# Causal attention with a bias table: the tiles of queries of a chunk of heads taken from the last to the first

## The chip, the cores and the metric

The kernel runs on one core of one Trainium2 chip. The metric is the time of one execution on the device, in microseconds (us). The core has five engines that run beside each other, each through its own list of instructions in order, and that wait for one another by counting semaphores: TensorE (PE in the profile, with its weight loads as PEld), ScalarE (ACT), VectorE (DVE), GpSimd (POOL) and SyncE (SP), which starts the transfers.

## The reference

The reference is a decoder of four layers over 4 sequences of 512 tokens of width 128. Each layer has an attention, a cross attention to 154 tokens of context and a feed-forward part, each followed by a layer norm. The change touches one of these twelve parts, the attention of the last layer (16 heads of width 8; the kernel runs it with a table for 512 positions):

```python
def _L3_attn_ref(x, WQ, bQ, WK, bK, WV, bV, WO, bO, rel_pos_table):
    q = (x @ WQ.T + bQ).reshape(b, t, N_HEADS, D_K).transpose(0, 2, 1, 3)
    k = (x @ WK.T + bK).reshape(b, t, N_HEADS, D_K).transpose(0, 2, 1, 3)
    v = (x @ WV.T + bV).reshape(b, t, N_HEADS, D_K).transpose(0, 2, 1, 3)
    scores = jnp.einsum('bhqd,bhkd->bhqk', q, k) / jnp.sqrt(jnp.float32(D_K))
    ...
    scores = scores + rel_bias.transpose(2, 0, 1)[None]
    causal = pos[None, :] <= pos[:, None]
    scores = jnp.where(causal[None, None], scores, -jnp.inf)
    attn = jax.nn.softmax(scores, axis=-1)
    out = jnp.einsum('bhqk,bhkd->bhqd', attn, v)
    out = out.transpose(0, 2, 1, 3).reshape(b, t, d)
    return out @ WO.T + bO
```

Because of the causal mask, a tile of 128 queries needs only the keys up to its own end: the first tile 128 keys, the second 256, the third 384, the last 512.

## The kernel before

The program loops twice over pairs of sequences. Within a pass it goes through the parts of the network, and each part is done for one sequence ("lane") and then for the other. The attention with the table (class `L3Attention`, lines 2181 to 2233) thus runs four times in an execution; each of these runs is called a stage below.

A stage first projects queries, keys and values (`pe_table`, line 338) and then runs an object of class `Attention` (line 465), which serves all the softmax attentions of the network. For this stage it has 16 heads in four chunks of four heads (`hpc` is 4: each head has a strip of 32 partitions), and four rounds for a chunk (`rpc` is 4), each with one tile of 128 queries (`nq` and `w` are 1). So there are 16 rounds, and a round has four items k = 0 to 3, one for each head. `width` (line 521) gives the keys of an item: 128 times the number of the query tile, counted from one.

The rounds are pipelined over 18 steps. In step i each engine does, in this order:

- PE: the scores of round i (line 561, each head into a PSUM bank of its own, the head's matmul waiting until VectorE has read that bank in the round before); at the first step past a chunk's last round the transposes of the reciprocals (line 572); the transposes of the probabilities of round i-1 (line 592), the four heads going through a ring of three PSUM banks, so that a head's transposes wait until the bank's last content has been copied out; the products with the values of round i-2 (line 610), all into bank O1.
- DVE: per head, scores plus bias, written to NB with the row minimum of the negated sum (line 719, which waits for the scores); between the heads' instructions the reciprocal of the sums (line 734) and the copies of two heads of round i-1 (line 640); at the end of the step behind a chunk's last products the multiplication of the chunk's output by the reciprocals (line 745), which waits for those products. PE's first products of the next chunk wait for it.
- ACT: per head the exponential (line 691, which also sums the row), and the copies of the other two heads of round i-1 (line 638); once a chunk the copy of the transposed reciprocals (line 647).
- POOL: the spreading of the reciprocals over the strips (line 656).

In rounds 0 and 1 PE issues a matmul whose result nobody reads just ahead of the first transposes (`warm=(0, 1)`, `idle` at lines 399 and 586). In step 1 DVE also does the layer norm of the sequence before (`beside`, line 2232), and in step 3 PE transposes the input of the next stage (`late={3: ["X"]}`, line 804), which ACT copies in step 4 (line 813). In the last step PE does the output projection of the first two chunks, then the last products, then the projection of chunks 3 and 4 (line 754).

The tile of queries of a round is `rd % self.rpc` in four places: `item` (line 518), the products (line 606), the spreading (line 651) and the reciprocal (line 733). So a chunk goes through 128, 256, 384 and 512 keys, and the next chunk starts again with 128.

Of the kernel before, what the change touches and what calls it, by code (L numbers as in the profile page):

```python
# [13 lines left out]
P = 128  # L14
NBATCH, SEQ, CTX = 4, 512, 154
# [185 lines left out]
def build(nc, io):  # L201
    ctx = ExitStack()
    with ctx:
# [261 lines left out]
        class Attention:  # L465
# [1 line left out]


            def __init__(self, heads, dh, nkeys, added=None, causal=False, keys=None, queries=None,
                         banks=None, split="ADDA", exes=None, late=None, warm=(), turn_first=True):  # L470
                self.heads, self.dh, self.nkeys, self.added, self.causal = heads, dh, nkeys, added, causal
                self.keys, self.queries = keys, queries
                self.ctx = nkeys == CTX
                self.kc = CK if self.ctx else P
                self.nch = nkeys // self.kc
                self.slot = {8: 32, 64: 64, P: P}[dh]
                self.hpc = P // self.slot
                self.chunks = heads // self.hpc
                self.w = 2 if self.ctx else 1
                self.nq = 4 * self.w // self.hpc  # L480
                self.rpc = NT // self.nq
                self.rounds = self.chunks * self.rpc
                self.banks = banks or PP3
                self.exes = exes or [EX[:, e, :] for e in range(4)] + [QT[:, 4 + e, :] for e in range(4)]
                self.steps = self.rounds + 2
                self.seq, self.first = [], []
                self.late = late or {}
                self.x_done = None
                self.warm = warm
                self.turn_first = turn_first  # L490
                self.late_at = {}
                done = {"A": 0, "D": 0}
                self.also(0)
                self.recip_at = []
                for rd in range(self.rounds + 1):
                    if rd >= 1 and rd % self.rpc == 0:
                        self.recip_at.append(len(self.seq))
                        done["A"] += 1
                        self.seq.append(("A", done["A"]))
                    self.first.append(len(self.seq))  # L500
                    for k in range(4 if rd < self.rounds else 0):
                        done[split[k]] += 1
                        self.seq.append((split[k], done[split[k]]))
                    self.also(rd + 1)
# [7 lines left out]
            def late_bank(self, j):  # L512
                return self.banks[self.late_at[j] % len(self.banks)]

            def item(self, rd, k):

                q, j = divmod(k, self.hpc)
                q0 = (rd % self.rpc) * self.nq + q * self.w
                return list(range(q0, q0 + self.w)), j

            def width(self, qts):
# [22 lines left out]
            def pe(self, pe, r, ready=(), beside=None, wo=None, fill=None, valued=(), late=None, fill_at=1):  # L544
                nb = len(self.banks)
                for i in range(self.steps):
                    if i == fill_at and fill:
                        fill(pe)
                    if i < self.rounds:
                        rd, c = i, i // self.rpc  # L550
# [47 lines left out]
                    if 0 <= rd < self.rounds:  # L598
                        c = rd // self.rpc
                        for k in range(4):  # L600
                            self.evacuated(pe, r, self.first[rd] + k)
                        if rd % self.rpc == 0 and c >= 1:
                            pe.wait_ge(r.av_sb, c)
                        for sem, count in valued if rd == 0 else ():
                            pe.wait_ge(sem, count)
                        q0 = (rd % self.rpc) * self.nq
                        last = q0 if self.causal else self.nch - 1
                        for kc in range(last + 1):
                            for j in range(self.hpc):
                                ins = pe.matmul(O1[self.slot * j:self.slot * (j + 1), q0 * P:(q0 + self.nq) * P],  # L610
                                                self.value(c * self.hpc + j, kc), self.probs(rd, j)[:, kc, :],
                                                start=(kc == 0), stop=(kc == last))
                        ins.then_inc(r.av, 1)
# [34 lines left out]

            def spread(self, pool, r, rd):

                c, q0 = rd // self.rpc, (rd % self.rpc) * self.nq
                pool.wait_ge(r.recip, rd + 1)
                if c >= 1:
                    pool.wait_ge(r.recipT, c)
                of = recips[:, self.column(c, q0, 0, self.nq * self.hpc)]
                pool.tensor_copy(RX[:, q0 * P:(q0 + self.nq) * P].rearrange("p (n s) -> p n s", s=self.slot),  # L656
                                 of.unsqueeze(2).broadcast_to([P, self.nq * self.hpc, self.slot])
                                 ).then_inc(r.spread, 1)
# [41 lines left out]
            def dve(self, dve, r, free=None, beside=None, late=None):  # L700
                for i in range(self.steps):
                    for j in self.late.get(i - 1, ()):
                        if j != "X":
                            late(dve, j)
                    for k in range(4):
                        if i < self.rounds:
                            rd = i
                            n = 4 * rd + k
                            qts, j = self.item(rd, k)
                            h, N = (rd // self.rpc) * self.hpc + j, self.width(qts)  # L710
                            dve.wait_ge(r.scores, n + 1)
                            if self.added and rd >= 1:
                                dve.wait_ge(r.exped, n - 3)
                            elif n >= 8:
                                dve.wait_ge(r.exped, n - 7)
                            at = 2 * (n % 8)
                            if self.added:
                                for a, qt in enumerate(qts):
                                    ins = dve.tensor_tensor_reduce(  # L719
                                        NB[:, k, a * N:(a + 1) * N], S4[k][:, a * N:(a + 1) * N],  # L720
                                        self.added(h, qt), -1.0, HUGE, ALU.add, ALU.min, neg[:, at + a:at + a + 1])
                            else:
                                ins = dve.tensor_reduce(neg[:, at:at + self.w],
                                                        S4[k][:, 0:self.w * N].rearrange("p (a k) -> p a k", k=N),
                                                        AX.X, ALU.max, negate=True)
                            ins.then_inc(r.negmax, 1)
                        if 1 <= i <= self.rounds and k >= 2:
                            rd, c = i - 1, (i - 1) // self.rpc
                            if k == 2:
                                dve.wait_ge(r.exped, 4 * rd + 4)  # L730
                                if c >= 2:
                                    dve.wait_ge(r.spread, (c - 1) * self.rpc)
                                of = self.column(c, (rd % self.rpc) * self.nq, 0, self.nq * self.hpc)
                                dve.reciprocal(recips[:, of], sums[:, of]).then_inc(r.recip, 1)  # L734
                                self.turn(dve, r, "D", rd, 0, free)
                                self.turn(dve, r, "D", rd, 1, free)
                            else:
                                self.turn(dve, r, "D", rd, 2, free)
                                self.turn(dve, r, "D", rd, 3, free)
                    rd = i - 2  # L740
                    if 0 <= rd < self.rounds and rd % self.rpc == self.rpc - 1:
                        c = rd // self.rpc
                        dve.wait_ge(r.av, rd + 1)
                        self.evacuated(dve, r, self.recip_at[c])
                        dve.tensor_tensor(self.out_chunk(c), O1[:, :], RS[:, c % 2, :], ALU.mult).then_inc(r.av_sb, 1)  # L745
                    if beside:
                        beside(i)
# [1433 lines left out]
        class L3Attention(LaneStep):  # L2181
            kind = 13

            def __init__(self, *a):
                LaneStep.__init__(self, *a)
                w, XT = self.w, self.L.XT
                self.att = Attention(16, 8, SEQ, causal=True, keys=lambda c: KT[:, c, :],
                                     added=lambda h, qt: relbias[:, h, SEQ - P * (qt + 1):SEQ], warm=(0, 1),
                                     late={3: ["X"]})
                rowsA = [([(w("wq")[:, c * P:(c + 1) * P], XT[:, :])], P, SEQ, "A", "act", QT[:, c, :],  # L2190
                          (ACT.Identity, scaled[:, 4 + c:5 + c], RSQRT8)) for c in range(4)]
# [363 lines left out]
```

## Time and profile before

| what | us |
|---|---|
| median of 3 runs | 4173.82 |
| lowest, highest run | 4170.47, 4176.15 |
| the profiled execution | 4180.67 |
| its span from first to last instruction | 4179.0 |
| busy in the span: PE, DVE, ACT, POOL | 3893.9, 2766.9, 1978.4, 948.6 |
| mean granted TensorE clock | 0.977 |

The profiled execution is a run of its own, 6.85 us above the median of the three. A time read from its rows is a place or a length within its span of 4179.0 us. PE's busy time counts a matmul from its start to its modelled end, and the matmuls overlap, so that a row such as "x8" with 1.09 us holds eight of them.

### The profile page before, as it was taken

How to read it: one execution, taken by the hardware profiler on the slowest of the kernel's cores; microseconds unless marked ns; L12 is line 12 of the kernel's file. 1: busy time of each engine (PE TensorE's matmuls, PEld its weight loads, DVE VectorE, ACT ScalarE, POOL GpSimd, SP SyncE). 2: the span in 40 equal slices, each digit the busy share in tenths (PEclk: the TensorE clock that was granted, in tenths of full speed). 3: DMA queues.
4: the chain of work that ended last, by engine and by line, in shares of the span. 5: the costliest groups of instructions: out<-in, count | busy, mean ns of one | idle time of the engine just before them, and what ended most of it. 6: DMA issues, size and time to landing. Idle time of an engine off the chain costs nothing. (4 is left out here: it accounts for less than half of the span.)

```text
span 4179.0 us, 70765 instructions
## 1 busy us (share of the span) xinstructions
PE 3893.9 (93%) x23508; PEld 2394.3 (57%) x23508; DVE 2766.9 (66%) x8036; ACT 1978.4 (47%) x5740; POOL 948.6 (23%) x1040
## 2 busy tenths in 40 slices
PE   7999899999999999999989998999999999999998
PEld 4644455665655655666646444565556556555665
DVE  3787767677767747664447886776777776476644
ACT  1732445655555533663228224555565555346722
POOL 0145332233322200000001462322323321000000
PEclk8999999999999999999979999999999999999999
DMA  1100000000000010000010000000000000201000
GB/s 57 43 17 1 17 7 18 24 17 24 17 24 2 26 58 21 31 37 9 4 59 6 17 1 17 7 17 24 18 24 17 24 2 26 72 7 56 12 9 11
DMA packets 15853, 91.87 MB, mean 22 GB/s; under 512 B 2176, under 2 KB 8064, under 8 KB 12032
## 3 DMA queue, kind: packets, MB, share of 16 engines
q1 hardware_dynamic: 15488, 87.27, 5.8%
q8 instruction: 196, 3.21, 0.3%
q14 instruction: 169, 1.38, 0.1%
HBM read 86.22 MB, written 1.05 MB: 21 GB/s over the span
## 5 line engine op out<-in xcount | busy, mean ns | idle before, releaser
L610 PE MATMUL ps_O<-wide,V 128*64 128x256 f32 (+4 forms) x5152 | 596.2, 393 | 1.9 <-ACT wide L638 1.9
L691 ACT ACTIVATE EX<-NB,neg 128x154 f32<-128x154 f32 (+3 forms) x768 | 402.7, 531 | 107.6 <-DVE neg L719 107.6
L561 PE MATMUL ps_S<-KT,QT 64*128 64x154 f32 (+7 forms) x1936 | 373.5, 456 | 59.9 <-POOL QT L1619 25.3
L656 POOL COPY RX<-recips 128x256 f32<-128x256 f32 (+2 forms) x356 | 156.6, 440 | 1127.9 <-DVE recips L734 1127.9
L745 DVE TENSOR_TENSOR QT<-ps_O,RS 128x512 f32<-128x512 f32 x212 | 146.5, 691 | 395.2 <-PE ps_O L610 394.6
L640 DVE COPY wide<-ps_P 128x512 f32<-128x512 f32 (+4 forms) x528 | 339.8, 647 | 75.2 <-PE ps_P L592 72.4
L610 PEld LDWEIGHTS ps_O<-wide,V 128*64 128x64 f32 (+4 forms) x5152 | 266.8, 127 | 194.6 <-issue 110.7
L429 POOL TENSOR_TENSOR small<-small 128x4 f32<-128x4 f32 x112 | 113.6, 1014 | 1065.6 <-DVE small L414 902.8
L561 PE MATMUL ps_T<-KT,QT 64*128 64x154 f32 (+5 forms) x968 | 322.2, 435 | 3.4 <-ACT EX L691 3.4
L561 PE MATMUL ps_OUT<-KT,QT 64*128 64x154 f32 (+5 forms) x968 | 325.2, 434 | 0.1
L592 PE MATMUL ps_P<-consts,EX 128*128 128x128 f32 (+1 forms) x1956 | 294.1, 286 | 25.9 <-ACT RS L647 13.0
L691 ACT ACTIVATE QT<-NB,neg 128x512 f32<-128x512 f32 (+2 forms) x512 | 311.8, 619 | 0.0
L561 PEld LDWEIGHTS ps_S<-KT,QT 64*128 64x128 f32 (+2 forms) x1936 | 159.2, 188 | 249.8 <-issue 163.0
L638 ACT ACTIVATE wide<-ps_P 128x512 f32<-128x512 f32 (+4 forms) x432 | 241.2, 558 | 124.7 <-PE ps_P L592 124.5
L592 PEld LDWEIGHTS ps_P<-consts,EX 128*128 128x128 f32 (+1 forms) x1956 | 226.6, 149 | 78.1 <-ACT RS L647 21.4
L592 PE MATMUL ps_P<-consts,QT 128*128 128x128 f32 (+1 forms) x1624 | 240.3, 280 | 24.5 <-DVE wide L640 11.1
L592 PEld LDWEIGHTS ps_P<-consts,QT 128*128 128x128 f32 (+1 forms) x1624 | 177.6, 143 | 87.6 <-issue 36.8
L638 ACT ACTIVATE wide<-ps_O 128x512 f32<-128x512 f32 (+2 forms) x280 | 160.1, 572 | 112.8 <-PE ps_O L592 112.8
L561 PEld LDWEIGHTS ps_OUT<-KT,QT 64*128 64x128 f32 (+2 forms) x968 | 155.2, 189 | 80.3 <-issue 68.0
L719 DVE CUSTOM_DVE_ANT_0 NB<-ps_S,maskb 128x512 f32<-128x512 f32 x256 | 165.9, 685 | 40.8 <-PE ps_S L561 40.8
L754 PEld LDWEIGHTS ps_OUT<-weights,QT 128*128 128x128 f32 x1536 | 178.3, 192 | 24.8 <-issue 24.8
L754 PE MATMUL ps_OUT<-weights,QT 128*128 128x128 f32 x1536 | 190.4, 278 | 0.0
(388 smaller groups left out, 8231.5 us busy)
## 6 DMA issues: line engine op xcount, KB each, us to landing
weights<-in_w_dram SPq DMA_DIRECT2D x10, 1664.0 KB, 6.9
weights<-in_w_dram SPq DMA_DIRECT2D x2, 6148.0 KB, 17.5
weights<-in_w5next_dram SPq DMA_DIRECT2D x6, 1664.0 KB, 6.9
weights<-in_w_dram SPq DMA_DIRECT2D x2, 4200.0 KB, 12.9
weights<-in_reltab_dram SPq DMA_DIRECT2D x2, 4096.0 KB, 14.1
weights<-in_w_dram SPq DMA_DIRECT2D x8, 640.0 KB, 3.9
weights<-in_w_dram SPq DMA_DIRECT2D x5, 832.0 KB, 4.5
weights<-in_w_dram SPq DMA_DIRECT2D x2, 2050.0 KB, 7.9
```

Source lines behind the costliest of these rows:

```text
L429: pool.tensor_tensor(small[:, 36:40], small[:, 32:36], small[:, half:half + 4], ALU.pow).then_inc(r.rstd, 1)
L561: ins = pe.matmul(S4[k][:, a * N:(a + 1) * N], QT[strip, c, qts[a] * P:(qts[a] + 1) * P], self.keys(c)[strip, 0:N], start=True, stop=True)
L592: ins = pe.transpose(self.banks[s % nb][0:self.kc, b * P:(b + 1) * P], ex[:, a * N + kc * self.kc:a * N + (kc + 1) * self.kc], ident)
L610: ins = pe.matmul(O1[self.slot * j:self.slot * (j + 1), q0 * P:(q0 + self.nq) * P], self.value(c * self.hpc + j, kc), self.probs(rd, j)[:, ...
L638: eng.activation(dst, src, ACT.Copy).then_inc(r.turned_act, 1)
L640: eng.tensor_copy(dst, src).then_inc(r.turned_dve, 1)
L656: pool.tensor_copy(RX[:, q0 * P:(q0 + self.nq) * P].rearrange("p (n s) -> p n s", s=self.slot), of.unsqueeze(2).broadcast_to([P, self.nq * ...
L691: ins = act.activation(ex[:, a * N:(a + 1) * N], src, ACT.Exp, bias=neg[:, at:at + 1], scale=-1.0 if self.added else 1.0, accum_out=sums[: ...
L719: ins = dve.tensor_tensor_reduce(NB[:, k, a * N:(a + 1) * N], S4[k][:, a * N:(a + 1) * N], self.added(h, qt), -1.0, HUGE, ALU.add, ALU.min ...
L745: dve.tensor_tensor(self.out_chunk(c), O1[:, :], RS[:, c % 2, :], ALU.mult).then_inc(r.av_sb, 1)
L754: ins = pe.matmul(OUT[:, t * P:(t + 1) * P], self.out_chunk(c)[:, t * P:(t + 1) * P], wo[:, c * P:(c + 1) * P], start=(c + t == 0), stop=( ...
```

## The change

`Attention` gets an option `down`. With it, round n of a chunk takes query tile 3-n in place of n: a chunk begins with the tile of 512 keys, goes on with 384 and 256 and ends with 128. The function `query` gives the tile to the four places that computed it, and `L3Attention` alone sets the option. The number of instructions, their sizes, the buffers, the waits and the order of the kinds of work in a step remain; only which round is how wide changes.

```diff
             def __init__(self, heads, dh, nkeys, added=None, causal=False, keys=None, queries=None,
-                         banks=None, split="ADDA", exes=None, late=None, warm=(), turn_first=True):
+                         banks=None, split="ADDA", exes=None, late=None, warm=(), turn_first=True,
+                         down=False):
...
+            def query(self, rd):
+
+                n = rd % self.rpc
+                return (self.rpc - 1 - n if self.down else n) * self.nq
+
             def item(self, rd, k):
 
                 q, j = divmod(k, self.hpc)
-                q0 = (rd % self.rpc) * self.nq + q * self.w
+                q0 = self.query(rd) + q * self.w
                 return list(range(q0, q0 + self.w)), j
...
-                        q0 = (rd % self.rpc) * self.nq
+                        q0 = self.query(rd)
                         last = q0 if self.causal else self.nch - 1
...
-                c, q0 = rd // self.rpc, (rd % self.rpc) * self.nq
+                c, q0 = rd // self.rpc, self.query(rd)
...
-                                of = self.column(c, (rd % self.rpc) * self.nq, 0, self.nq * self.hpc)
+                                of = self.column(c, self.query(rd), 0, self.nq * self.hpc)
...
                 self.att = Attention(16, 8, SEQ, causal=True, keys=lambda c: KT[:, c, :],
-                                     added=lambda h, qt: relbias[:, h, SEQ - P * (qt + 1):SEQ], warm=(0, 1),
+                                     added=lambda h, qt: relbias[:, h, SEQ - P * (qt + 1):SEQ], warm=(0, 1), down=True,
                                      late={3: ["X"]})
```

## Rows read from the trace of the kernel before

**Rows 1.** Stage two: stretch, us, busy PE, PEld, DVE, ACT, POOL, clock, DMA.

```profile
1704.88:1768.12 63.24, 58.86 (x666) 38.89 (x667) 46.75 (x185) 49.20 (x165) 4.69 (x16) 1.00 0.01 2
```

**Rows 2.** The same view for one chunk in the middle of stage one.

```profile
1652.23:1666.28 14.05, 13.01 (x160) 8.34 (x164) 11.21 (x45) 12.10 (x42) 1.17 (x4) 1.00 0.00 1
```

**Rows 3.** Who waited for whom in that chunk: us in total, times, longest.

```profile
PEld ps_P L592 <- ACT wide L638: 1.0, 2, 0.8
DVE NB L719 <- PE ps_T L561: 1.0, 1, 1.0
DVE QT L745 <- PE ps_O L610: 0.9, 1, 0.9
```

**Rows 4.** Timeline of that chunk, PE: start, us, engine, line, instruction, count.

```profile
1652.09 0.59 PE L561 MATMUL ps_S<-KT,QT 32*128 32x384 f32 x2
...
1652.95 0.44 PE L592 MATMUL ps_P<-consts,QT 128*128 128x128 f32 x2
...
1654.23 0.43 PE L610 MATMUL ps_O<-wide,V 128*32 128x128 f32 x8
...
1654.59 0.70 PE L561 MATMUL ps_S<-KT,QT 32*128 32x512 f32 x2
...
1658.14 0.64 PE L610 MATMUL ps_O<-wide,V 128*32 128x128 f32 x16
1658.72 0.38 PE L561 MATMUL ps_S<-KT,QT 32*128 32x128 f32 x2
...
1659.28 1.09 PE L592 MATMUL ps_P<-consts,QT 128*128 128x128 f32 x8
...
1661.92 0.86 PE L610 MATMUL ps_O<-wide,V 128*32 128x128 f32 x24
...
1662.72 0.48 PE L561 MATMUL ps_S<-KT,QT 32*128 32x256 f32 x2
...
1663.36 0.66 PE L572 MATMUL ps_P<-consts,RX 128*128 128x128 f32 x4
...
1665.13 1.08 PE L610 MATMUL ps_O<-wide,V 128*32 128x128 f32 x32
1666.14 0.59 PE L561 MATMUL ps_S<-KT,QT 32*128 32x384 f32 x2
```

**Rows 5.** The same timeline, DVE: scores plus bias of 512 and of 256 keys.

```profile
1655.75 0.69 DVE L719 CUSTOM_DVE_ANT_0 NB<-ps_S,weights 128x512 f32<-128x512 f32 x1
...
1656.36 0.68 DVE L719 CUSTOM_DVE_ANT_0 NB<-ps_S,weights 128x512 f32<-128x512 f32 x1
...
1663.45 0.42 DVE L719 CUSTOM_DVE_ANT_0 NB<-ps_S,weights 128x256 f32<-128x256 f32 x1 [1.03 <-PE ps_T L561]
```

**Rows 6.** Timeline of stage two's start: first scores, unread matmul, first chunk's multiplication.

```profile
1704.88 0.38 PE L561 MATMUL ps_S<-KT,QT 32*128 32x128 f32 x2 [0.43 <-issue]
...
1707.10 1.12 PE L402 MATMUL ps_P<-consts 128*128 128x512 f32 x2
...
1708.06 0.38 PE L592 MATMUL ps_P<-consts,EX 128*128 128x128 f32 x2
...
1724.10 0.69 DVE L745 TENSOR_TENSOR QT<-ps_O,RS 128x512 f32<-128x512 f32 x1 [0.90 <-PE ps_O L610]
```

**Rows 7.** Busy time in stage one from third to fourth multiplication, and behind it.

```profile
1680.33:1694.34 14.01, 13.28 (x153) 8.91 (x154) 8.29 (x27) 9.04 (x26) 0.88 (x3) 1.00 0.00 1
1694.34:1696.25 1.91, 1.91 (x17) 1.91 (x18) 1.28 (x2) 0.00 (x0) 0.00 (x0) 1.00 0.00 0
```

**Rows 8.** Busy time and clock, first scores to first multiplication: stages two, one, three, four.

```profile
1704.88:1724.10 19.22, 17.64 (x188) 11.37 (x192) 14.76 (x67) 15.97 (x58) 1.46 (x5) 1.00 0.01 3
1631.86:1652.23 20.37, 18.94 (x188) 11.84 (x192) 14.64 (x67) 15.94 (x58) 1.46 (x5) 0.92 0.01 2
3713.24:3733.51 20.27, 18.80 (x188) 11.49 (x192) 14.58 (x67) 15.85 (x58) 1.46 (x5) 0.92 0.01 2
3786.17:3806.99 20.82, 19.39 (x188) 12.09 (x192) 14.76 (x67) 15.97 (x58) 1.46 (x5) 0.92 0.01 2
```

More of the change, by code:

```diff
@@ L490, in __init__ @@
                 self.turn_first = turn_first
+                self.down = down
                 self.late_at = {}
```

## The prediction

> **What bounds the kernel now.** I read the busy time over whole stages first. Stage two takes 63.24 us from its first scores to the end of its projection [rows 1]; there are four such stages in the execution, and outside them the program is the same. Next I read a single chunk. In its steady state a chunk takes 14.05 us, and in it PE is busy for 13.01, ACT for 12.10 and DVE for 11.21 [rows 2]. PE's figure counts matmuls that overlap, so what PE issues has to be taken from the starts of its groups. Then the waits: none is long, but they sit on different engines, 1.0 us of DVE for scores, 0.9 of DVE for the chunk's last products, 1.0 of PE's weight loads for a copy by ACT [rows 3]. So no engine is full, and the period is a ring in which each engine waits a little for the next. Last the timeline of PE, which gives each step its length. I write a step as (scores; transposes; products) in tiles of 128 keys. From one first scores matmul to the next, (3;2;1) takes 2.50 us, (4;3;2) 4.13, (1;4;3) 4.00 and (2;1;4) 3.42, which sums to 14.05 [rows 4].
>
> **The parts of a step, from rows.** Scores hold PE for 0.64 us at two tiles (1662.72 to 1663.36) and 0.86 at three (1652.09 to 1652.95), 0.22 a tile; so 0.43 at one and 1.08 at four. Transposes cost 0.11 each (eight in 1.09, of which the last one's tail is 0.2). Products take 0.36, 0.58, 0.80 and 1.01 us for one to four tiles (to the next first scores) [rows 4]. DVE starts on scores of four tiles 1.16 us after they start, and goes on every 0.61 us [rows 4, 5]; its result counts 0.7 us after its start.
>
> **The change, part by part.** Nothing is removed or added: the same instructions of the same sizes run in another order of rounds. The steps become (4;1;2), (3;4;1), (2;3;4), (1;2;3). POOL and the transfers have nothing on this path: POOL is busy for 1.17 us of a chunk [rows 2], and no DMA of a stage moves. I lay each step out along PE.
>
> - (4;1;2): scores 1.08, four transposes 0.44, a wait of 0.5 for a copy by ACT before the fourth head's transposes may use the ring (the kind in [rows 3]), products 0.58. Sum 2.60.
> - (3;4;1): each head's scores need DVE to have read the four-tile scores of the same head. The last of these reads starts 1.22 (1.16 and the semaphore) + 3 x 0.61 + 0.27 (a reciprocal and a one-tile copy between them) after the four-tile scores began, and counts 0.74 later: 4.06, so 1.46 into this step. Then 0.86 scores, 0.55 transposes of the reciprocals, 1.90 for 16 transposes with two short waits, 0.36 products. Sum 5.13. This is the step that gets worse: the wide reads of DVE stand bare here, while before PE met them with the transposes of three tiles.
> - (2;3;4): scores 0.72, twelve transposes and a wait for ACT's copy 2.07, products 1.01. Sum 3.80.
> - (1;2;3): scores 0.45, eight transposes with a wait 1.24, products 0.80. Sum 2.49.
>
> The chunk sums to 14.02 us, against 14.05 [rows 2]. Two full periods lie between a stage's first and third multiplication, so they give 0.06 us back.
>
> Start of a stage. Before, 19.22 us lie between the first scores and the first multiplication, at full clock [rows 6, 8]. After: DVE has read the last four-tile scores at 1.22 + 3 x 0.61 + 0.74 = 3.79; three-tile scores 0.86, to 4.65; the unread matmul 0.96 (1707.10 to 1708.06 in [rows 6]), to 5.61; 16 transposes 1.90, to 7.51; two-tile scores, behind a 0.44 wait for DVE, which has the four-tile copies to make, to 8.59; unread matmul to 9.55; twelve transposes 1.56 and products 1.01, to 12.12; (1;2;3) with the four transposes of the next stage's input 2.93, to 15.05; (4;1;2) to 17.65; (3;4;1) to 22.78; multiplication 0.54 later, 23.32. This costs 4.10 us a stage.
>
> End of a stage. Before, the third and fourth multiplications are 14.01 us apart and the projection ends 1.91 later [rows 7]. After, counted from the third multiplication: the step (2;3;4) began 0.54 earlier, so 3.80 - 0.54 = 3.26; (1;2;3) 2.49; one-tile transposes with their waits 1.07, products of two tiles 0.58; reciprocals 0.44; half the projection 1.87; the last products, now of one tile, and the step over to DVE 0.54. Sum 10.25, which gives back 3.76 us. What follows the multiplication stays 1.91.
>
> A stage: +4.10 - 0.06 - 3.76 = +0.28 us, four of them +1.1 us. The long start is paid by the short end, since a pipeline's start costs its first rounds and its end its last ones, and the sizes only swap places.
>
> The clock. In stage two the granted clock stays at 1.00 (2.4 GHz) during the start; in the other three it falls to 1.2 GHz for a part of it (mean 0.92), and these starts take 20.37, 20.27 and 20.82 us against 19.22, so a fall costs 1.15, 1.05 and 1.60, 3.8 us in all [rows 8]. PE ran short bursts of scores just before. After the change PE has scores alone for 4.65 us, with 0.9 us of nothing in them, so I take falls in three or four stages. At half clock the unread matmul (0.96) and the 16 wide transposes (1.76) may double: a fall costs between 1.05, the cheapest row, and 2.7; I take 1.7, nearest to the dearest row. 3.5 x 1.7 - 3.8 = +2.2 us.
>
> Sum: +1.1 + 2.2 = +3.3 us. On the profiled span 4179.0 becomes 4182.3, with the 1.67 us around it 4184.0; that execution lies 6.85 above the median, and the median of 4173.82 becomes 4177.
>
> **The rivals.** F, faster. The chunk's end is what binds the ring: DVE waits 0.90 us for the chunk's last products [rows 6] and then 1.03 for scores [rows 5]. The last products shrink from 1.01 to 0.36 us, and in my working the multiplication no longer waits. If this were the path, 0.9 us for each of 16 chunks would go: 14.4, 4159. Against it: in the new order DVE waits instead for the one-tile scores behind the four-tile products (0.8) and for the four-tile scores (1.6), so the idle moves.
>
> S, slower, by the clock. The fall does not stay at the stage's start. In (3;4;1) PE again has little but scores, held apart by DVE's reads, for some 2.3 us. If that brings the clock down once in every chunk, 16 falls at the mean of the three rows, 1.27, make 20.3 in place of 3.8: +16.5 + 1.1, 4191. For it: the three falls at the starts. Against it: the one-tile and two-tile transposes and products run between, and the chunk before keeps 1.00 throughout [rows 2]. It decides as soon as the low stretch recurs in each chunk. The Trainium skill, page "TensorE: Matmul & The Clock Gate", section "HAM oscillation", says that a loop whose waits recur in each pass can have its clock lowered in each pass. By that rule S would hold; the trace of before agrees for starts only.
>
> T, slower: the end gives nothing back, because ACT or DVE and not PE ends it: then +3.76 x 4 = 15.0 on top of 3.3, 4192. Against it: behind the last multiplication PE is busy for 1.91 of 1.91 us [rows 7], and ACT has no work there.
>
> **How the numbers follow.** Forecast 0.68, F 0.12, S 0.13, T 0.07. The forecast's own range is 4168 to 4186: half a microsecond to one and a half on each stage for the waits that I only estimated, and 1.05 to 2.7 for a fall in two to four stages. A measurement of this kernel can tell about 0.2% from no change, 8.3 us. The forecast gives 0.01 faster, 0.59 the same and 0.08 slower; F gives faster; S and T give slower but for a fall in only a few chunks, which stays within. Range 4166 to 4192. Faster 0.13, same 0.60, slower 0.27.
>
> **What would show each step.** Multiplications (line 745) 14.0 us apart within a stage; the first 23.3 us (full clock) behind the first scores; the fourth 10.25 behind the third; steps of 2.6, 5.1, 3.8 and 2.5 us. DVE's 0.90 wait ahead of line 745 gone, and a wait of some 1.6 us ahead of the first four-tile read of a chunk. Whole stages of 63.5 to 66 us. I would be wrong if the period differs by more than 0.3 us, for there are twelve of them, or if the granted clock in mid-stage is below 1.00.

## The result and the profile after

The changed kernel takes 4186.21 us (median of 13 runs, 4178.07 to 4194.06) against 4173.82 before (13 runs, 4164.34 to 4182.62). The ratio is 1.003, with a 95% interval from 1.0021 to 1.004: slower by 0.2 to 0.4%. Timed a second time it was 1.0021 (1.0011 to 1.0031). The forecast was 4177 with a range of 4166 to 4192, and "within 0.2%" as the likeliest case. The time lies in the whole range, 9 us above the point and on the slower side of the bound, but at the very edge of what the forecast itself allowed (4168 to 4186): the room up to 4192 came from the rivals S and T.

Busy time over the four stages in the profile after. Columns: stretch, us, busy time of PE, PEld, DVE, ACT and POOL with their instructions, granted clock, share of DMA, GB/s.

```profile
1629.13:1695.14 66.01, 63.06 (x665) 41.14 (x666) 45.70 (x185) 49.77 (x165) 4.73 (x16) 0.95 0.01 2
1703.77:1769.96 66.19, 63.19 (x666) 41.22 (x667) 45.80 (x185) 49.82 (x165) 4.73 (x16) 0.95 0.01 2
3721.61:3787.57 65.96, 63.00 (x665) 41.19 (x666) 45.73 (x185) 49.72 (x165) 4.73 (x16) 0.95 0.01 2
3796.20:3862.42 66.22, 63.25 (x666) 41.20 (x667) 45.79 (x185) 49.81 (x165) 4.73 (x16) 0.95 0.01 2
```

They sum to 264.4 us. In the first profile of the kernel before, the four stages took 64.39, 63.24, 64.30 and 64.83, together 256.8 ([rows 1] is the second of them). So the stages account for +7.6 of the +11.4 us between the two spans, 4190.4 and 4179.0. The rest lies in parts that the change does not touch. ACT, DVE and POOL are busy for as long as before within 1 us; PE is busy for longer, and its mean clock is 0.95 in all four stages.

The same view from the first scores to the first multiplication (line 745 of before, 752 of after), stage two first, for [rows 8]:

```profile
1703.77:1729.89 26.12, 25.03 (x204) 15.18 (x204) 17.29 (x68) 18.05 (x56) 1.48 (x5) 0.87 0.01 2
1629.13:1655.08 25.95, 24.91 (x204) 15.13 (x204) 17.22 (x68) 18.00 (x56) 1.47 (x5) 0.87 0.00 1
3721.61:3747.51 25.90, 24.85 (x204) 15.18 (x204) 17.26 (x68) 17.94 (x56) 1.48 (x5) 0.87 0.00 1
3796.20:3822.34 26.14, 25.09 (x204) 15.20 (x204) 17.27 (x67) 18.04 (x56) 1.48 (x5) 0.87 0.01 2
```

Then one period, the way from the third to the fourth multiplication and what follows it, all of stage two, for [rows 2, 7]:

```profile
1729.89:1743.81 13.92, 13.31 (x163) 8.45 (x156) 10.91 (x47) 12.23 (x42) 1.19 (x4) 1.00 0.01 2
...
1757.73:1768.05 10.32, 9.64 (x140) 7.23 (x134) 5.40 (x27) 7.32 (x28) 0.89 (x3) 1.00 0.01 2
1768.05:1769.97 1.92, 1.92 (x18) 1.92 (x19) 1.29 (x2) 0.00 (x0) 0.00 (x0) 1.00 0.00 0
```

The period of 13.92 us, the short end of 10.32 and the unchanged 1.92 are what the steps gave (14.02, 10.25, 1.91). The start is not: 26 us against 23.3. The timeline of PE shows the steps of the period by their first scores, for [rows 4], and that of DVE its two longest waits for scores and the multiplication without a wait, for [rows 5]:

```profile
1729.41 0.48 PE L568 MATMUL ps_S<-KT,QT 32*128 32x256 f32 x2
...
1733.20 0.38 PE L568 MATMUL ps_S<-KT,QT 32*128 32x128 f32 x2
...
1735.71 0.70 PE L568 MATMUL ps_S<-KT,QT 32*128 32x512 f32 x2
...
1738.32 0.91 PE L568 MATMUL ps_S<-KT,QT 32*128 32x384 f32 x4
...
1743.33 0.48 PE L568 MATMUL ps_S<-KT,QT 32*128 32x256 f32 x2
```

```profile
1733.72 0.29 DVE L726 CUSTOM_DVE_ANT_0 NB<-ps_S,weights 128x128 f32<-128x128 f32 x1 [0.79 <-PE ps_T L568]
...
1736.87 0.69 DVE L726 CUSTOM_DVE_ANT_0 NB<-ps_S,weights 128x512 f32<-128x512 f32 x1 [1.48 <-PE ps_T L568]
...
1743.81 0.68 DVE L752 TENSOR_TENSOR QT<-ps_O,RS 128x512 f32<-128x512 f32 x1
```

The steps take 3.79, 2.51, 2.61 and 5.01 us. Last, the start of stage two in PE's timeline, for [rows 6], and the clock of 6.7 us in it:

```profile
1703.77 0.70 PE L568 MATMUL ps_S<-KT,QT 32*128 32x512 f32 x2 [0.43 <-issue]
...
1709.11 2.07 PE L402 MATMUL ps_P<-consts 128*128 128x512 f32 x2
...
1710.98 1.92 PE L599 MATMUL ps_P<-consts,EX 128*128 128x128 f32 x8
...
1714.53 0.48 PE L568 MATMUL ps_S<-KT,QT 32*128 32x256 f32 x2
...
1715.17 1.13 PE L402 MATMUL ps_P<-consts 128*128 128x512 f32 x2
```

```profile
1707.70:1714.40 6.70, 6.70 (x21) 4.29 (x20) 2.84 (x11) 3.30 (x11) 0.29 (x1) 0.50 0.00 1
```

The unread matmul comes 5.34 us behind the first scores (worked out: 4.65), the transposes at 7.21 (5.61) and the next scores at 10.76 (7.51). Of these 3.25 us, 0.44 are won back, since the wait for DVE that my steps had among these scores is gone. From the second unread matmul on (11.40, worked out 8.59) the distance to my steps is 2.8 us and stays. All of the loss lies in a stretch that PE spends at half clock.

### The profile page after: what moved, and what is told of

The parts are those of the page before. It is cut to its first block and busy times, and to the rows that moved or that the text cites. A ratio compares the mean times of both kernels' runs of the same rounds, so it can differ in the third digit from the quotient of the medians.

```text
span 4190.4 us, 70765 instructions
## 1 busy us (share of the span) xinstructions
PE 3908.6 (93%) x23508; PEld 2401.7 (57%) x23508; DVE 2764.0 (66%) x8036; ACT 1982.3 (47%) x5740; POOL 950.2 (23%) x1040
## 3 DMA queue, kind: packets, MB, share of 16 engines
HBM read 86.22 MB, written 1.05 MB: 21 GB/s over the span
## 5 line engine op out<-in xcount | busy, mean ns | idle before, releaser
L698 ACT ACTIVATE EX<-NB,neg 128x154 f32<-128x154 f32 (+2 forms) x768 | 416.5, 549 | 113.7 <-DVE neg L726 113.7
L599 PE MATMUL ps_P<-consts,EX 128*128 128x128 f32 (+1 forms) x2048 | 307.9, 289 | 22.4 <-ACT RS L654 9.2
L698 ACT ACTIVATE QT<-NB,neg 128x512 f32<-128x512 f32 (+3 forms) x512 | 298.1, 592 | 0.0
L599 PEld LDWEIGHTS ps_P<-consts,EX 128*128 128x128 f32 (+1 forms) x2048 | 241.0, 150 | 68.5 <-issue 21.5
L599 PE MATMUL ps_P<-consts,QT 128*128 128x128 f32 (+1 forms) x1536 | 231.0, 281 | 23.5 <-DVE wide L647 11.1
L645 ACT ACTIVATE wide<-ps_O 128x512 f32<-128x512 f32 (+3 forms) x280 | 159.4, 569 | 113.1 <-PE ps_O L599 112.2
```

The source lines that it names most:

```text
L599: ins = pe.transpose(self.banks[s % nb][0:self.kc, b * P:(b + 1) * P], ex[:, a * N + kc * self.kc:a * N + (kc + 1) * self.kc], ident)
L645: eng.activation(dst, src, ACT.Copy).then_inc(r.turned_act, 1)
L698: ins = act.activation(ex[:, a * N:(a + 1) * N], src, ACT.Exp, bias=neg[:, at:at + 1], scale=-1.0 if self.added else 1.0, accum_out=sums[: ...
```

## The experiments

Theory C: the start is longer than the steps say because the granted clock is at 1.2 GHz for 6.8 us there. Rival D: waits for DVE and ACT make it longer, and the clock is a bystander. The other runs test the terms of the sum, the start, the end and the joins, one at a time. "Stages" is the sum of the four stages in the run's own profile.

| kernel | median, us | ratio to before (95%) | stages, us |
|---|---|---|---|
| before, again (x_before) | 4175.19 | 1.0003 (0.9992 to 1.0013) | 255.6 |
| changed (first series) | 4186.21 | 1.0030 (1.0021 to 1.0040) | 264.4 |
| changed, again (x_after) | 4183.50 | 1.0021 (1.0011 to 1.0031) | 263.5 |
| changed, four unread matmuls more (x_keep) | 4188.37 | 1.0034 (1.0021 to 1.0047) | 266.9 |
| changed, one unread matmul more (x_fill) | 4170.33 | 0.9989 (0.9980 to 0.9998) | 255.4 |
| changed, without unread matmuls (x_nowarm) | 4169.11 | 0.9985 (0.9975 to 0.9996) | 252.4 |
| first chunk down only (x_first) | 4186.89 | 1.0026 (1.0015 to 1.0038) | 266.6 |
| last chunk down only (x_last) | 4166.67 | 0.9981 (0.9972 to 0.9991) | 244.8 |
| up, down, up, down (x_zigzag) | 4151.17 | 0.9953 (0.9940 to 0.9965) | 237.4 |
| x_zigzag, one half-size unread matmul more (x_zigfill) | 4148.31 | 0.9940 (0.9926 to 0.9954) | 234.7 |
| x_zigfill, without the unread matmuls of rounds 0 and 1 (x_zigbare) | 4150.35 | 0.9944 (0.9924 to 0.9964) | 230.9 |
| before, without unread matmuls (x_upbare) | 4170.44 | 0.9986 (0.9975 to 0.9997) | 252.6 |

**Four unread matmuls (x_keep).** In `Attention.pe`, ahead of the wait of line 559:

```diff
+                                    if rd == 1 and self.down:
+                                        n = SEQ if k == 0 else SEQ // 2
+                                        pe.matmul(self.banks[0][:, 0:n], ident, K("cos")[:, 0:n], start=True, stop=True)
```

> The changed kernel with unread matmuls put between the scores of round 1 (one of 512 columns ahead of the first head's, one of 256 ahead of each other head's), so that PE does not stand still while DVE reads the wide scores. Theory C (the start of a stage is 2.7 us longer than my 23.3 because the granted clock is at half for 6.8 us there): the clock stays at 1.00 in the start, the first multiplication comes 23.5 to 24.5 us behind the first scores instead of 26.0, a stage takes about 64.2 instead of 66.1, and the kernel 8 us less than the changed one, near 4178. Rival D (the start is long by the waits for DVE and ACT themselves, and the clock is a bystander): the clock comes back, but the first multiplication stays at 26 us or later, since matmuls were only added, and the time stays at 4186 or above.

In three of the four stages the clock stayed at 1.00, and the start still took 25.96 us, as D has it. But the edit was no clean test of D. PE's timeline of stage two shows that the full-width matmuls keep the heads' scores from running beside each other:

```profile
1629.18:1657.97 28.79, 28.60 (x212) 16.43 (x212) 17.47 (x67) 18.04 (x56) 1.46 (x5) 0.88 0.00 1
1706.66:1732.62 25.96, 25.77 (x212) 14.60 (x212) 17.35 (x67) 17.93 (x56) 1.46 (x5) 1.00 0.01 2
```

```profile
1708.79 0.91 PE L571 MATMUL ps_S<-KT,QT 32*128 32x384 f32 x2
1709.63 0.70 PE L567 MATMUL ps_P<-consts 128*128 128x256 f32 x2
1710.26 0.91 PE L571 MATMUL ps_S<-KT,QT 32*128 32x384 f32 x2
1711.10 0.70 PE L567 MATMUL ps_P<-consts 128*128 128x256 f32 x2
```

Head follows head every 1.47 us, where DVE alone would let them go every 0.61. What the clock gave back, the added work took, so the 25.96 us say nothing for D. The first stage (the upper of the two windows) speaks for C: it had a fall of 6.8 us in spite of the added matmuls, and with the same instructions its start took 2.83 us longer than the other three.

**One unread matmul (x_fill).** Only the one that falls into a wait of PE is kept:

```diff
+                                    if rd == 1 and k == 0 and self.down:
+                                        idle(pe, self.banks[0])
```

> The changed kernel with a single unread matmul of 512 columns added, ahead of the first head's scores of round 1, where PE stands still for 0.85 us at full clock; nothing is added between the other heads' scores. Theory C (half clock makes the start 2.8 us longer than the steps say): the clock no longer falls for 6.8 us in the start, or for 3.4 at most, the first multiplication comes 23.3 to 23.7 us behind the first scores where the clock stays at 1.00, and a stage takes 63.6 to 64 there in place of 66.1; with all four so, -8 to -10 us against the changed kernel, 4176 to 4178. Rival D (waits make it, the clock is a bystander): the clock stays up and the first multiplication still comes at 26 us.

```profile
1703.04:1726.30 23.26, 23.07 (x206) 13.72 (x206) 17.17 (x68) 17.93 (x56) 1.46 (x5) 1.00 0.01 2
1630.04:1654.54 24.50, 24.31 (x202) 15.26 (x206) 17.25 (x67) 18.60 (x58) 1.46 (x5) 0.93 0.00 1
3749.00:3764.20 15.20, 14.58 (x159) 10.01 (x156) 11.00 (x46) 12.78 (x44) 1.17 (x4) 0.89 0.01 2
```

```profile
1704.11 1.12 PE L402 MATMUL ps_P<-consts 128*128 128x512 f32 x2
...
1707.71 1.12 PE L402 MATMUL ps_P<-consts 128*128 128x512 f32 x2
1708.67 1.04 PE L601 MATMUL ps_P<-consts,EX 128*128 128x128 f32 x8
...
1710.54 0.48 PE L570 MATMUL ps_S<-KT,QT 32*128 32x256 f32 x2
```

The edit only adds work on PE, and yet the start shrinks from 26 to 23.26 us in three of the four stages: C holds and D falls. The added matmul puts the next scores only 0.13 us later (2.13 us behind the first scores, 2.00 in the changed kernel), since it stands in a wait. The unread matmul of round 0 stands at 4.67 us behind the first scores, the transposes at 5.63 and the next scores at 7.50, where my steps had 4.65, 5.61 and 7.51. Two of the four stages took 63.32 us at full clock. The other two had one fall of 3.4 us each, not ahead of the first transposes but later, at 20 and at 48 us behind the first scores, and took 64.37. The second row of the windows is the start with the first of these, 24.50 us; the last row is the other, a period of 15.20 us instead of 13.91.

**No unread matmuls (x_nowarm)**, in `L3Attention`:

```diff
-    warm=(0, 1), down=True,
+    warm=(), down=True,
```

> The changed kernel without the two unread matmuls of rounds 0 and 1. They took 1.87 us at half clock and 0.97 at full clock, and in the changed order both stand on PE's path. If they only cost (theory C, with the low stretch where it was): the first multiplication comes at 23.2 to 23.5 us instead of 26.1, the kernel is 10 us below the changed one, 4176. If they are what brings the clock back (the low stretch gets longer without them): 24.5 to 27 us. Rival D, in which PE waits there for DVE and ACT anyway: 25.5 to 26 us with an unchanged low stretch.

```profile
1696.79:1720.25 23.46, 22.42 (x200) 14.65 (x200) 17.35 (x68) 18.05 (x56) 1.46 (x5) 0.85 0.01 2
1625.47:1648.10 22.63, 21.58 (x200) 13.71 (x200) 17.16 (x67) 18.04 (x56) 1.46 (x5) 0.92 0.01 1
```

All four starts still have a fall, of 6.8 us in two stages and of 3.4 in the other two, and they take 2.5 to 3.5 us less than in the changed kernel. So in this order the two matmuls stand on PE's path and did not keep the clock up. They came after the stretch in which PE had only scores. No start of this run was at full clock, so what they cost there is not shown by it (x_zigbare against x_zigfill below: 0.9 us, 19.87 against 20.79, in the other order).

**The first chunk alone (x_first)**, with `query` asking whether the chunk is in a list, and `down=(0,)`:

```diff
-                return (self.rpc - 1 - n if self.down else n) * self.nq
+                return (self.rpc - 1 - n if rd // self.rpc in self.down else n) * self.nq
```

> The kernel before with only the first chunk of each stage from 512 down to 128, the other three up. It has the changed start and the old end. Working by steps at full clock: first multiplication 19.9 us behind the first scores (0.7 more than before), periods 14.05 and 14.01 as before, so +0.7 a stage, about +3 us. Theory C adds the long half-clock stretch: 2.7 us on each start against about 1.0 before: first multiplication near 22.5, +2.3 to +2.9 a stage, 4183 to 4186. Rival D: the start is slower by waits alone, first multiplication also above 22 us but with the clock at 1.00.

```profile
1706.55:1729.11 22.56, 21.15 (x188) 13.24 (x192) 14.40 (x68) 15.54 (x55) 1.46 (x5) 0.85 0.01 2
```

All four starts took 22.5 to 22.8 us with a fall of 6.8 us in each, 2.6 to 2.9 above the 19.9 of the steps (which no run measured at full clock), the periods 14.05 and the ends 14.0. Turning the first chunk alone is enough to bring the long fall. It is not the only way to one: two starts of x_upbare below have it with narrow first rounds.

**The last chunk alone (x_last)**, with the same `query`:

```diff
-    warm=(0, 1), down=True,
+    warm=(0, 1), down=(3,),
```

> The kernel before with only the last chunk of each stage from 512 down to 128. It has the old start and the changed end. By the steps: the join of two rounds of 512 keys costs 1.4 us (third multiplication 15.5 behind the second in place of 14.05), the fourth follows 10.1 to 10.3 later in place of 14.01, net -2.4 us a stage, -9 to -10 us: 4164. Under rival T (the end gives nothing back) the kernel would stay at 4174 or above; the trace of the changed kernel speaks against T already.

```profile
1662.74:1678.04 15.30, 15.26 (x172) 9.86 (x176) 14.10 (x45) 14.04 (x43) 1.19 (x4) 1.00 0.01 2
1678.04:1688.18 10.14, 9.88 (x141) 7.43 (x142) 5.29 (x26) 7.13 (x26) 0.89 (x3) 1.00 0.01 2
```

The join of two rounds of 512 keys costs 1.25 us, the end gives back 3.9, and the kernel is faster by 0.1 to 0.3%. The gain at the end is real and does not hang on the start.

**Up, down, up, down (x_zigzag)**, with the same `query`:

```diff
-    warm=(0, 1), down=True,
+    warm=(0, 1), down=(1, 3),
```

> Chunks one and three up (128 to 512), chunks two and four down (512 to 128): the old start, the changed end, two joins of 512 to 512 keys and one of 128 to 128. By the steps the first multiplication is at 20.9 (its chunk's last step stands beside wider scores), then 10.4, 15.5 and 10.1: about 58.7 us a stage at full clock against 63.2, so -4 to -4.6 a stage and -16 to -18 us: 4156 to 4158. If joins cost more than the steps say, or the clock falls at them, -8 us or less.

```profile
1624.70:1645.50 20.80, 19.98 (x200) 12.88 (x204) 17.36 (x68) 18.01 (x58) 1.46 (x5) 1.00 0.01 2
1645.50:1656.00 10.50, 9.85 (x148) 6.67 (x152) 8.05 (x46) 9.62 (x39) 1.17 (x4) 1.00 0.01 2
1656.00:1671.29 15.29, 15.25 (x172) 9.85 (x176) 14.09 (x45) 14.56 (x46) 1.17 (x4) 1.00 0.01 3
1671.29:1681.43 10.14, 9.89 (x141) 7.43 (x142) 5.30 (x27) 7.12 (x26) 0.88 (x3) 1.00 0.01 2
```

The rows meet the steps (20.9, 10.4, 15.5, 10.1) to 0.2 us each, and the kernel beats both the one before, by 0.35 to 0.6%, and the changed one. Two of its four starts had a fall of 3.4 us and took 22.1 us instead of 20.8. Here both ends of a stage meet a small round, and the turning points are 512 to 512 and 128 to 128 instead of 512 to 128.

**Two variants of it (x_zigfill, x_zigbare).** The first adds an unread matmul of 256 columns ahead of round 1's first scores, the second has that one and drops those of rounds 0 and 1.

```diff
+                                    if rd == 1 and k == 0 and self.down:
+                                        pe.matmul(self.banks[0][:, 0:256], ident, K("cos")[:, 0:256], start=True, stop=True)
...
-    warm=(0, 1), down=(1, 3),
+    warm=(), down=(1, 3),
```

> The kernel with chunks one and three up and two and four down, plus an unread matmul of 256 columns ahead of the first head's scores of round 1. Where the clock fell for 3.4 us in the start (two stages of four) a stage took 1.3 us more than where it did not (60.0 against 58.7). Theory C: no fall in the four starts, every stage 58.7 to 58.9, some 2 us less in the four together, too little for the timed ratio: 4149 to 4151. If the fill costs more than it saves: 59.2 or more in each stage.

> Chunks up, down, up, down, with the added unread matmul of 256 columns ahead of round 1 but without the two of rounds 0 and 1. With them the four stages took 58.6 to 58.7 us with the clock at 1.00. Path theory: 0.7 to 1.0 us less each where the clock stays up, 57.7 to 58.0, so 4144 to 4146. Clock theory: one or more of the four starts has a fall of 3.4 or 6.8 us, stages of 59 to 60 there, and nothing is gained: 4148 to 4152.

```profile
1692.36:1751.07 58.71, 57.39 (x668) 38.96 (x669) 46.32 (x185) 49.35 (x165) 4.74 (x16) 1.00 0.01 2
```

```profile
1630.30:1688.02 57.72, 56.59 (x663) 38.59 (x664) 45.86 (x185) 49.23 (x165) 4.69 (x16) 1.00 0.01 2
```

None of these eight stages had a fall: 58.6 to 58.7 us each, then 57.7. The three intervals of this order overlap, so the timed runs do not rank them.

**The kernel before without unread matmuls (x_upbare).**

```diff
-    added=lambda h, qt: relbias[:, h, SEQ - P * (qt + 1):SEQ], warm=(0, 1),
+    added=lambda h, qt: relbias[:, h, SEQ - P * (qt + 1):SEQ], warm=(),
```

> The kernel before (all chunks up) without its two unread matmuls. In the changed order taking them away gave 2.5 to 3.4 us a stage. In the old order the steps say: the first matmul stands between the scores of round 1 and the first transposes, the second partly beside a wait for DVE, so at full clock 0.5 to 0.8 us a stage; if a start then has the 6.8 us fall as in the changed kernel, +1.5 in place of it. Path theory: 3 us faster, 4171. Clock theory (they earn their place by keeping the clock up in the old order): the falls get longer, stages at 65 or more, 4177 or above.

```profile
1631.45:1651.09 19.64, 18.25 (x184) 11.70 (x188) 14.50 (x68) 15.97 (x58) 1.48 (x5) 0.83 0.01 2
3712.44:3730.99 18.55, 17.01 (x184) 11.35 (x188) 14.39 (x67) 15.97 (x58) 1.48 (x5) 0.91 0.01 2
```

The falls did get longer (6.8 us in two stages, 3.4 in the others), and still no start took more than 19.64 us, where before they took 19.2 to 20.8. The path theory was nearer, in time and size; of the clock theory only the longer falls came.

**The controls (x_before, x_after)**, the two kernels without an edit.

> The kernel before once more, as a control of the comparison: ratio 1.000 with an interval of about 0.001 to each side, periods 14.05, ends 14.0 and 1.9, stages of 63.2 without and 64.3 to 64.8 with a fall of the clock in the start. How many of the four starts have a fall is open (three in the first profile); it tells how much of the stages' +7.6 us between the two first profiles is chance: 1.2 us for each.

> The changed kernel once more. The four stages took 7.6 us more than in the first profile of the kernel before and 8.8 more than in its second, while the medians are 12 us apart; this run tells whether the remaining 3 to 4 us are chance. If the stages are all: ratio 1.0020, about 4182, and a second profile with 66.0 to 66.2 us in each stage and 3917 to 3922 outside them. If something outside the stages is slower too: ratio 1.003 again and 3925 or more outside them.

The kernel before, run again, had two falls in its four starts, where its first profile had three, and stages of 255.6 us. The changed kernel, timed again, came to 1.0021. Three of its starts had the 6.8 us fall and took 25.8 to 27.0 us, one had 3.4 us and took 24.6:

```profile
3791.81:3816.42 24.61, 23.57 (x204) 14.56 (x204) 17.17 (x67) 17.93 (x56) 1.47 (x5) 0.93 0.01 2
```

So the start grows with the length of the fall: 23.26 us without one (x_fill), 24.6 with 3.4 us, 26.0 with 6.8. The start of 27.0 us, in the third stage, had a second fall of 3.4 us on top. The stages sum to 263.5 us, and the time outside them was 3921 us, as in the other profiles (3908 to 3926).

## Why the prediction was right or wrong

**The order of the steps.** Right, term by term. At full clock (x_fill) the start took 23.26 us (23.32 worked out), the period 13.91 (14.02), the end 10.32 (10.25), the rest 1.91. Against before that is +4.04, two times -0.14 and -3.69, so +0.1 us a stage: 63.32 against 63.24, where I had +0.28. "The long start is paid by the short end" holds to a tenth of a microsecond at full clock. One slip in the signs of being wrong: there are not twelve periods but eight, two in each stage; the third distance is the end.

**The step that gets worse.** (3;4;1) took 5.01 us, against 5.13. DVE's 0.90 us wait for the last products is gone, and 1.48 and 0.79 us of waiting for scores stand in its place (I had 1.6 and 0.8). So rival F was a shift of idle time, as argued: the period fell by 0.13 us and not by 0.9.

**The clock, the term that was mis-sized.** I expected falls in three or four stages at 1.7 us each, 6.0 in all. They came in all four of the first profile at 26.03 - 23.26 = 2.8 us each, 11.1 in all. The range I gave for one fall, 1.05 to 2.7, ended just below that. I took the value nearest to the dearest row of before, 1.60, but those rows were falls of 3.4 us over narrow transposes, and after the change a fall lasts 6.8 us and covers the unread matmul (1.87 instead of 0.96) and the 16 wide transposes with their waits (3.55 instead of 1.90). Both were named in the prediction as what "may double"; the value should have gone to that end. Comparisons within one kernel agree: 2.83 us for 6.8 us of half clock in x_keep, and 1.2 to 1.4 us between a fall of 3.4 and one of 6.8 in x_after. With 11.1 in place of 6.0 the sum is 0.4 + 11.1 - 3.8 = +7.7, which is the +7.6 of the stages.

**From the stages to the median.** The first series has 12.4 us between the medians, the second 10.8, and the ratio of the second, 1.0021, is +8.8. The stages give 7.6 to 8.8, by which profile of before is taken. The interval of the second series (4.6 to 12.9 us) holds these, that of the first (8.8 to 16.7) only at its edge. In the second profile nothing outside the stages was slower (3921 us, against 3922 and 3918 in the two of before), so chance is the likely source of the remainder, but no run shows it.

**The rival S.** As stated, one fall in every chunk, it did not come: the first profile has none in mid-stage. A weak form did. One chunk of the second profile and two in the profile of x_fill had a fall of 3.4 us, which made their stages 0.8 to 1.1 us longer. All three began inside a step (3;4;1), right behind its three-tile scores, which is the step that S named. In x_fill, from those scores to just ahead of the fall, and then in it:

```profile
1647.81:1650.20 2.39, 2.39 (x13) 1.03 (x10) 2.39 (x10) 2.38 (x9) 0.29 (x1) 1.00 0.00 0
1650.30:1653.60 3.30, 3.30 (x18) 3.30 (x17) 1.41 (x7) 2.28 (x6) 0.29 (x1) 0.50 0.00 0
```

So the place was right, and what was wrong in S is that it would happen in every chunk. The second sign of being wrong, a granted clock below 1.00 in mid-stage, did come in these two profiles, though not in the first.

The rule of the Trainium skill, page "TensorE: Matmul & The Clock Gate", section "HAM oscillation", that a loop with recurring waits can be lowered in each pass, is met here by the starts and by these few chunks only. The page's own case is a loop in which PE stands still for a transfer in each pass, and this kernel is no such loop.

**The rival T.** Refuted by the end of 10.32 us and by x_last, where the end was changed alone.

**The chances.** "Within 0.2%" at 0.60 was too much. With the fall at its upper price in all four stages the forecast itself would have stood at +8, on the bound. That the measured time still fell into the range 4166 to 4192 is in part luck: its upper end was set by two rivals that did not come, and the forecast's own range ended at 4186.

## What to carry to other kernels

In this pipeline over rounds of unequal size the start costs its first rounds and the end its last ones. Turning the whole order round only swaps these two; an order that begins and ends small, and turns at equal sizes in between, won 4.6 us a stage at full clock. Before pricing a start, look for the stretch in which TensorE has nothing but short, spread matmuls, and give the work behind it a price at half clock too: all 16 starts that began with 512 keys and had nothing put ahead of round 1 had a fall there. A single unread matmul placed into a real wait ahead of that work can be worth more than it costs, while one on the path is paid in full.

## What the runs showed of the hardware

An added matmul can shorten a kernel: one of 512 columns (1.06 us with its issue) ahead of round 1 took the clock from 0.87 to 1.00 and the start from 26 to 23.26 us in three stages of four. With an unread matmul at this place one start in 16 had a fall there (in x_keep; eight of the 16 began with 128 keys). Where it stands decides: the unread matmuls of rounds 0 and 1, behind the stretch of scores, did not prevent the fall, and taking them away saved 2.5 to 3.5 us a stage. Matmuls of four heads on strips of 32 rows run beside each other (four heads of 512 keys within 1.07 us), but a full-width matmul between them puts them in a row, 1.47 us a head. And the granted clock fell to 1.2 GHz right behind a stretch in which PE was busy by its row for 2.88 of 3.73 us:

```profile
1703.77:1707.50 3.73, 2.88 (x14) 1.19 (x14) 2.49 (x9) 1.75 (x5) 0.00 (x0) 1.00 0.02 4
```

That is the stretch of the changed kernel just ahead of the fall. All that PE ran in it were scores on strips of 32 rows. Whether it was their strips, their spacing or their number that brought the fall, no run separates.
